# Cross attention computed head by head in 64x64 blocks, and the normalisations moved from VectorE to ScalarE, in a one-core decoder kernel

## What is computed

```python
# self attention, 16 heads of 8 channels, polynomial instead of softmax
att = einsum('bhid,bhjd->bhij', q, k) / sqrt(8); att = where(causal, att, -inf)
att = polymax(att)
x = layernorm(x + (att @ v) @ W_proj)
# cross attention to a context, 16 heads of 64 channels
q = (x @ WQ); k = (ctx @ WK); v = (ctx @ WV)          # 128 -> 1024 each
weights = softmax(einsum('nqhk,nlhk->nhql', q, k) / sqrt(64))
x = layernorm(x + einsum('nhqk,nkhv->nqhv', weights, v).reshape(n, 64, 1024) @ WO + bO)
# 16 experts, the best 6 of them weighted by a router
x = layernorm(x + sum_e gate[:, e] * (x @ expert_w[e]))
```

## Time and profile before

| | |
|---|---|
| median of 3 runs | 1194.37 us (1193.98 to 1194.49) |
| the profiled execution, whole | 1193.11 us |
| its span, first to last instruction | 1191.2 us |
| TensorE busy | 1122.3 us (94%) |
| VectorE busy | 1036.7 us (87%) |
| ScalarE busy | 706.8 us (59%) |
| GpSimd busy | 364.3 us (31%) |
| mean granted TensorE clock | 0.984 of full speed |

### The profile page before, as it was taken

How to read it: one execution, slowest core, us unless ns; L and a number is a source line. 1 busy time by engine, 2 the same in 40 slices (tenths; PEclk the granted TensorE clock), 3 DMA queues, 4 the chain that set the end, 5 groups by cost and what they waited for, 6 DMA issues and landing times.

```text
span 1191.2 us, 31777 instructions
## 1 busy us (share of the span) xinstructions
PE 1122.3 (94%) x9856; PEld 851.6 (71%) x9856; DVE 1036.7 (87%) x3341; ACT 706.8 (59%) x1418; POOL 364.3 (31%) x489
## 2 busy tenths in 40 slices
PE   3989999999999999999999999999999999999964
PEld 3767777777777777777777777777777777777643
DVE  4669998989899988989998898999898999889667
ACT  3766665566675555676555566655666665556420
POOL 3232233232323233232323323332323232332221
PEclk9999999999999999999999999999999999999978
DMA  4232333332233332233333223333322333321230
GB/s 147 59 79 55 94 94 80 92 79 52 67 92 92 79 92 66 52 80 92 92 79 92 56 52 90 92 83 89 83 52 63 92 92 79 92 72 44 63 76 9
DMA packets 49998, 92.09 MB, mean 77 GB/s; under 512 B 6576, under 2 KB 28592, under 8 KB 49968
## 3 DMA queue, kind: packets, MB, share of 16 engines
q1 hardware_dynamic: 49968, 91.70, 31.6%
HBM read 20.37 MB, written 4.19 MB: 21 GB/s over the span
## 4 chain that ended last, share of the span: by engine, by line
PE 56%; DVE 25%; issue 11%; POOL 3%; ACT 2%; DMA 1%; SPq 1%; DVEq 1%; POOLq 0%; ACTq 0%
PE ps_B L370 45%; DVE sums L776 13%; PE ps_S L370 5%; PE ps_B L487 5%; DVE p L723 3%; DVE x L707 3%; POOL rstd L910 2%; DVE ps_B L776 2%; DVE stats L688 1%; DMA vb<-vb_raw 1%; PE ps_B L457 1%; DVE rowmax L719 1%; SPq L354 1%; DVE mv L694 1%; POOL rstd L908 1%
## 5 line engine op out<-in xcount | busy, mean ns | idle before, releaser
L555 ACT ACTIVATE z<-ps_B 128x512 f32<-128x512 f32 x256 | 149.9, 601 | 212.2 <-PE ps_B L370 208.4
L776 DVE SCALAR_TENSOR_TENSOR sums<-ps_B,gate,sums 128x128 f32<-128x128 f32 x896 | 239.5, 341 | 1.4 <-PE ps_B L370 1.4
L915 POOL TENSOR_TENSOR p<-p,rowinv 128x1024 f32<-128x1024 f32 x64 | 122.0, 1906 | 308.6 <-DVE rowinv L732 308.6
L555 ACT ACTIVATE vb_raw<-ps_B 128x512 f32<-128x512 f32 x256 | 155.4, 607 | 88.6 <-PE ps_B L370 69.3
L370 PE MATMUL ps_B<-cT_hi,a_hi 128*128 128x256 f32 x512 | 157.0, 307 | 0.0
L370 PE MATMUL ps_B<-cT_lo,a_hi 128*128 128x256 f32 x512 | 144.2, 282 | 0.0
L370 PE MATMUL ps_B<-cT_hi,a_lo 128*128 128x256 f32 x512 | 144.1, 281 | 0.0
L370 PE MATMUL ps_S<-z,x1T 128*64 128x512 f32 x512 | 126.3, 614 | 10.1 <-DVE p L723 9.5
L370 PE MATMUL ps_B<-ex_hi,x2T_hi 128*128 128x512 f32 x256 | 114.6, 448 | 18.2 <-DVE sums L776 15.4
L370 PEld LDWEIGHTS ps_B<-cT_hi,a_hi 128*128 128x128 f32 x512 | 96.8, 189 | 44.9 <-issue 25.3
L908 POOL TENSOR_TENSOR rstd<-mv,ln_eps_tile 128x2 f32<-128x2 f32 x96 | 18.9, 197 | 337.2 <-DVE mv L694 336.8
(11 more groups left out here) (106 smaller groups left out, 2466.3 us busy)
## 6 DMA issues: line engine op xcount, KB each, us to landing
vb<-vb_raw SPq DMA_DIRECT2D x256, 256.0 KB, 4.3
xT<-in_x_t SPq DMA_DIRECT2D x32, 256.0 KB, 2.6
cT<-in_ctx_t SPq DMA_DIRECT2D x32, 128.0 KB, 2.3
x_sb<-in_x SPq DMA_DIRECT2D x32, 128.0 KB, 3.5
out<-x SPq DMA_DIRECT2D x32, 128.0 KB, 4.1
staging<-in_wq_t SPq DMA_DIRECT2D x1, 512.0 KB, 4.7
staging<-in_wk_t SPq DMA_DIRECT2D x1, 512.0 KB, 5.8
staging<-in_wv_t SPq DMA_DIRECT2D x1, 512.0 KB, 6.7
```

Source lines behind the costliest of these rows:

```text
L555: return nc.scalar.activation(dst, src, ACT.Copy, scale=scale)
L776: done = V.scalar_tensor_tensor(after, ps[BANK[f"FF{4 * r + q}"]][:, C * e:C * e + C], gate[:, r, 4 * q + e:4 * q + e + 1], before, ALU.mu ...
L915: G.tensor_tensor(weights, weights, rowinv[:, r].unsqueeze(2).broadcast_to([P, H, T]), ALU.mult).then_inc(p2_ready, 1)
```

## The change

Nothing is folded any more. Six jobs `heads` transpose WQ, WK and WV once and split them (`heads_hi`, `heads_lo`). For a tile, four jobs `Q2_` form the queries of all heads from `x1T_hi`, `x1T_lo` (stage `l1`), four jobs `K2_` the keys from the context (`l1`), and four jobs `V2_` the values (now in `l2`). The scores are one product for each head and sequence, with 64 channels, 64 queries and 64 keys; the probability product is one for each head and sequence too, and the two sequences' results go to two banks (`AC0a` and `AC0b`). ScalarE moves those four banks to `oT`, and `WO0`, `WO1` multiply by WO. The copies by DMA (`place`) are gone.

ScalarE now does the three `norm` steps as scale and bias; GpSimd's `root` gets two more small instructions for the bias. `x1T` is split by ScalarE (`x1_hi`) and VectorE (`x1_lo`). The value product of self attention writes only the halves that are used. All five orders are new. The diff, cut to its core:

```diff
 ACT_ORDER = """
-    K queries_hi VB6 Y exp0 VB1 Z7 Z2 relu0 relu1 square0 VB3 exp1 VB2 Z5 VB7 PT0a V PT0b square1 Z1 Z0 relu2 Z6
-    relu3 X1T square2 PT1a PT1b square3 VB5 base3 Z4 VB4 X2T Z3 VB0 logit_exp product_hi0 ...
+    Y K queries_hi V2_2 V exp0 V2_3 norm1 V2_0 V2_1 x1_hi exp1 relu0 relu1 K2_0 square0 Q2_0 K2_3 K2_2 PT0a square1
+    relu2 PT0b Q2_2 square2 PT1a PT1b relu3 Q2_1 AC0b square3 AC0a base3 AC1a AC1b norm2 K2_1 X2T Q2_3 logit_exp
+    norm3 heads_hi0 ...
...
 def v():
     for b in range(NB):
-        last = mm(ps[BANK["V"]][:, C * b:C * b + C], xT[:, b].rearrange("p a t -> p (a t)"), w_attn_sb[:, 2 * C:3 * C])
+        for par in range(2):
+            last = mm(ps[BANK["V"]][64 * par:64 * par + 64, T * b:T * b + T], xT[:, b, 0], w_v[:, par])
...
-def vb_part(n):
-    r, par, q = n // 4, n // 2 % 2, n % 2
-    return mm3(ps[BANK[f"VB{n}"]][:], cT_hi[:, rows], cT_lo[:, rows], vo_hi[:, par, cols], vo_lo[:, par, cols])
+def heads_of(what, n, hi, lo):
+    for k in range(2):
+        cols = slice(P * (2 * n + k), P * (2 * n + k) + P)
+        last = mm3(ps[BANK["QKV"[what] + f"2_{n}"]][:, TOK * k:TOK * k + TOK], heads_hi[:, what, cols], heads_lo[:, what, cols], hi[:], lo[:])
+def v2_part(n):
+    rows, cols = slice(P * (n // 2), P * (n // 2) + P), slice(512 * (n % 2), 512 * (n % 2) + 512)
+    return mm3(ps[BANK[f"V2_{n}"]][:], cT_hi[:, rows], cT_lo[:, rows], heads_hi[:, 2, cols], heads_lo[:, 2, cols])
 def s2(r):
-    for q in range(2):
-        for h in range(2):
-            b = 2 * r + h
-            last = mm(ps["S"][64 * h:64 * h + 64, 512 * q:512 * q + 512], x1T[:, T * b:T * b + T],
-                      z[:, b, 8 * q:8 * q + 8].rearrange("p h t -> p (h t)"))
+    pe.sem_inc(heads_begun, 1)
+    for c in range(4):
+        for bpar in range(2):
+            seq = slice(T * (2 * r + bpar), T * (2 * r + bpar) + T)
+            for z in range(2):
+                for e in range(2):
+                    j, cols = 2 * c + z, 512 * e + P * c + T * bpar
+                    last = mm(ps["S"][64 * z:64 * z + 64, cols:cols + T], q2T[64 * e:64 * e + 64, j, seq], k2T[64 * e:64 * e + 64, j, seq])
 def ac(r):
+    pe.sem_inc(heads_begun, 1)
+    for c in range(J):
+        for z in range(2):
+            for bpar in range(2):
+                h = 4 * (c % 4) + 2 * z + c // 4
+                done = mm(ps[own[bpar]][64 * z:64 * z + 64, T * c:T * c + T], v2[64 * bpar:64 * bpar + 64, r, DK * h:DK * h + DK],
+                          p2T[64 * bpar:64 * bpar + 64, r, c, T * z:T * z + T])
+def wo_turn(r):
+    for c in range(J):
+        last = mm(ps[BANK["WO1"]][:, C * r:C * r + C], oT[:, r, c], wo_sb[:, c], c == 0, c == J - 1)
...
+def norm(n):                                  # on ScalarE
+    act.wait_ge(ln_shift[n - 1], tile + 1)
+    for r in range(NR):
+        last = nc.scalar.activation(dst[:, r], rows_of(n, r), ACT.Identity, bias=shift[:, n - 1, r:r + 1], scale=rstd[:, n - 1, r:r + 1])
...
-def norm(n):                                  # on VectorE
-    dve.wait_ge(ln_rstd[n - 1], tile + 1)
-    for r in range(NR):
-        last = V.tensor_scalar(dst[:, r], rows_of(n, r), mv[:, n - 1, r, 0:1], rstd[:, n - 1, r:r + 1], ALU.subtract, ALU.mult)
+def x1T_low():
+    V.scalar_tensor_tensor(x1T_lo[:], ps[BANK["X1T"]][:, 0:TOK], 1.0, x1T_hi[:].bitcast(F32), ALU.mult, ALU.subtract)
...
 def root(n):
     G.tensor_tensor(rstd[:, n - 1], mv[:, n - 1, :, 1], ln_eps_tile[:], ALU.add).then_inc(ln_eps[n - 1], 1)
+    G.tensor_tensor(minus_mean[:, n - 1], mv[:, n - 1, :, 0], minus[:], ALU.mult).then_inc(ln_eps[n - 1], 1)
     G.tensor_tensor(rstd[:, n - 1], rstd[:, n - 1], power[:], ALU.pow).then_inc(ln_rstd[n - 1], 1)
+    G.tensor_tensor(shift[:, n - 1], minus_mean[:, n - 1], rstd[:, n - 1], ALU.mult).then_inc(ln_shift[n - 1], 1)
```

More of the change, by code:

```diff
@@ L81 @@
 SP_ORDER = """
-    x_columns context place1 place0 store x_rows
+    x_columns x_rows store context
 """.split()
 ACT_ORDER = """
-    K queries_hi VB6 Y exp0 VB1 Z7 Z2 relu0 relu1 square0 VB3 exp1 VB2 Z5 VB7 PT0a V PT0b square1 Z1 Z0 relu2 Z6
-    relu3 X1T square2 PT1a PT1b square3 VB5 base3 Z4 VB4 X2T Z3 VB0 logit_exp product_hi0 product_hi1 product_hi2
-    product_hi3 product_hi4 product_hi5 product_hi6 product_hi7
+    Y K queries_hi V2_2 V exp0 V2_3 norm1 V2_0 V2_1 x1_hi exp1 relu0 relu1 K2_0 square0 Q2_0 K2_3 K2_2 PT0a square1
+    relu2 PT0b Q2_2 square2 PT1a PT1b relu3 Q2_1 AC0b square3 AC0a base3 AC1a AC1b norm2 K2_1 X2T Q2_3 logit_exp
+    norm3 heads_hi0 heads_hi1 heads_hi2 heads_hi3 heads_hi4 heads_hi5
 """.split()
 DVE_ORDER = """
[L90 to L94, removed]
+    row_max0 gate2 less_max0 gate3 gate4 projected keys_lo0 gate5 stats1 keys_lo1 var1 queries_lo row_max1 less_max1
+    row_sum0 x1_lo row_inv0 row_sum1 gate6 allow0 row_inv1 pieces0 p1_0 gate7 allow1 gate8 pieces1 allow2 p1_1
+    pieces2 gate9 p1_2 gate10 gate11 gate12 allow3 gate13 pieces3 gate14 p1_3 gate15 weigh0 weigh1 attended stats2
+    var2 weigh2 weigh3 logits stats3 gate0 var3 gate1 heads_lo0 heads_lo1 heads_lo2 heads_lo3 heads_lo4 heads_lo5
 """.split()
 POOL_ORDER = """
-    context_hi context_lo shares0 shares1 root1 root2 next_x_hi bias_x1 next_x_lo x2_hi x2_lo root3 experts_hi
+    root1 next_x_hi context_hi context_lo shares0 shares1 root2 bias_x1 next_x_lo x2_hi root3 x2_lo experts_hi
     experts_lo
@@ L240, in decoder @@
         base3_ready, out_done = sem("base3_ready"), sem("out_done")
-        ln_stats, ln_var, ln_eps, ln_rstd = ([sem(f"ln{n}_{what}") for n in (1, 2, 3)] for what in ("stats", "var", "eps", "rstd"))
-        N_WEIGHTS = 16 * 8
+        ln_stats, ln_var, ln_eps, ln_rstd, ln_shift = ([sem(f"ln{n}_{what}") for n in (1, 2, 3)] for what in ("stats", "var", "eps", "rstd", "shift"))
+        N_WEIGHTS = 16 * (7 + 4)
         def wait(eng, s, n):
@@ L341, in x_columns @@
                         load(xT, x_t, xT_in, u + 1)
[L343 to L354, removed]
                 def store():
@@ L387, in body, with heads, heads_split @@
                 u, t, f = i + 2, i + 1, i - 1
-                def product(n):
+                def heads(n):
                     pe.wait_ge(w_in, N_WEIGHTS)
-                    what, par, q = n // 4, n % 2, n // 2 % 2
-                    rows = slice(64 * par, 64 * par + 64)
-                    left_w, right_w = ((wk_ld, wq_ld), (wv_ld, wo_ld))[what]
                     for k in range(4):
-                        cols = slice(C * (4 * q + k), C * (4 * q + k) + C)
-                        last = mm(ps[BANK[f"product{n}"]][:, C * k:C * k + C], left_w[rows, cols], right_w[rows, cols])
-                    return last
[L401 to L405, removed]
+                        j = 4 * (n % 2) + k
+                        last = pe.transpose(ps[BANK[f"heads{n}"]][:, P * k:P * k + P], heads_ld[n // 2][:, P * j:P * j + P], ident)
+                    return last
+                def heads_split(what):
+                    if isinstance(i, int) and i <= 0:
+                        for n in (2 * what, 2 * what + 1):
+                            wait_emptied(pe, -2, f"heads{n}")
                 def q():
@@ new lines, in s2 @@
+                def s2(r):
+                    wait_moved(f"S2_{r}", i - 1, last_of(ACT_ORDER, [f"Q2_{n}" for n in range(4)]), last_of(ACT_ORDER, [f"K2_{n}" for n in range(4)]))
+                    pe.sem_inc(heads_begun, 1)
[6 more added lines that the diff above has]
+                                    last = mm(ps["S"][64 * z:64 * z + 64, cols:cols + T], q2T[64 * e:64 * e + 64, j, seq], k2T[64 * e:64 * e + 64, j, seq])
@@ L526, in body @@
                         continue
[L528 to L530 removed]
+                    if job == "WO0":
+                        wait(pe, emptied[BANK["WO1"]], earlier(i, "WO1"))
+                    elif job != "WO1":
                         wait(pe, emptied[bank], earlier(i, job))
[L532 to L540 removed]
+                    if job[:2] == "AC":
+                        if job[3] == "b":
+                            ac(int(job[2]))
+                        continue
+                    if job[:2] == "S1":
                         if int(job[3:]) % PARTS == PARTS - 1:
@@ L543, in body @@
                         continue
+                    if job in work:
+                        last = work[job]()
+                    elif job[:2] == "PT":
+                        last = p2_turn(int(job[2]), "ab".index(job[3]))
                     else:
-                        last = ff(int(job[2:]))
+                        last = numbered[job.rstrip("01234567")](int(job[-1]))
                     if bank:
@@ L603, in move_p2T @@
                     move(job, p2T[:, r, 4 * q:4 * q + 4].rearrange("p j n -> p (j n)"), ps[BANK[job]][:])
-                def move_vb(n):
-                    r, par, q = n // 4, n // 2 % 2, n % 2
-                    if f"VB{n}" == first_of(ACT_ORDER, [f"VB{k}" for k in range(4 * r, 4 * r + 4)]):
-                        if not (isinstance(i, int) and t == 0):
```

(4 more changed lines are left out.)

187 lines of the change are left out of this document (85 added, 102 removed), and 23 rows, old and new, of the table JOBS.

## The result

The changed kernel takes 1145.6 us in the median of four runs, against 1194.2 for the kernel before: a ratio of 0.960, with a 95% interval of 0.958 to 0.962. The forecast was 1120 us. So the sign and the range (1080 to 1205) held, and the gain was 49 us where 74 were expected; the likeliest case's own range, 1085 to 1145 us, was just missed. One of the twelve runs of experiment e1, at 1207.7 us, was in a slower state and is left out of its median.

A forecast was written before the change was run, and what follows sets the result against it. TensorE was taken to bound the 35.0 us turn, VectorE close behind; TensorE's terms gave 31.95, plus 0.4 wait and 0.4 by choice, 32.75. Times 32 that is minus 72, setup minus 2: 1120 us, range 1080 to 1205.

The forecast's parts named there:

- the likeliest case: Whole kernel: the forecast itself, 1120 us, with 1085 to 1145 us as its own range; chance 0.62.
- The distance of the 64x64 rows: TensorE's score and probability products: 16.1 ns a row taken, saving 1.68 and 1.59 us a turn.
- two quadrants: Rival on TensorE: only two quadrants overlap, 28.5 ns a small row, 35.5 us a turn, about 1210 us; chance 0.10.
- a floor: Rival on TensorE: small rows have a floor above `Y`'s, 22.3 ns midway, 1160 to 1180 us; chance 0.08.
- no overlap: Rival on TensorE: small rows take 55 ns each, 42.3 us a turn, 1428 us; chance 0.04.
- WO and the values: TensorE, per turn: new WO products plus 3.52 us; four value jobs for eight context jobs minus 2.77.
- the loop: Third `var`, `root`, `norm3`, ScalarE to `square3`, VectorE's `pieces3` and `weigh`, next third `var`: 31.9 us if ScalarE never waits.
- The sum: Per turn: TensorE 31.95 + 0.4, VectorE 32.2, loop 31.9; with 0.4 added, 32.75 us, 2.25 less.
- a new wait: TensorE before `X1T`, for `norm1` on ScalarE behind `Y`, keys and queries: at least 0.2 us, taken as 0.4.
- 0.4 added by choice: Allowance of 0.4 us a turn, because three bounds so near each other will not all be met.
- the rival in which ScalarE's loop binds: Two microseconds of gaps in ScalarE's loop give 34.0 us a turn, about 1160 us; chance 0.12, and 0.04 beyond 1197.
- the two signs of being wrong: TensorE waiting for ScalarE's moves over 2 us a turn, or VectorE idle before `pieces` for a square.

The follow-up runs named there:

- e1: The changed kernel with the third normalisation one turn later in ScalarE's order, behind the next turn's queries; 1194.9 us, ratio 1.002 to the kernel before.
- e8: The changed kernel with two more small GpSimd operations in the third normalisation's `root`, the value unchanged; 1162.4 us, ratio 0.975 to the kernel before.
- e5: The changed kernel with only two of the eight terms of each WO product; 1119.0 us, ratio 0.938 to the kernel before.
- e1b: The changed kernel with the third normalisation behind the next turn's queries and the output store one turn later too; 1139.0 us, ratio 0.956.
- e4: The changed kernel with score and probability products ordered quadrant by quadrant instead of changing quadrant each time; 1403.9 us, ratio 1.177 to the kernel before.

## Why the prediction was right in direction, and where its size was off

*The distance of the 64x64 rows: right.* 16.1 ns was taken, with 14 and 55 as ends; measured up to the next job it is 17. Both jobs of scores and both of probabilities take 1.09 to 1.19 us, 4.46 a turn for 7.39: minus 2.93 where minus 3.27 was expected. A job takes 0.06 us more than `Y`'s 1.03, measured the same way, and the one ahead of `Y`, whose blocks have another size, 0.16 more. The rivals with two quadrants, with a floor and with no overlap did not happen. The Trainium skill's floor (TensorE: Matmul & The Clock Gate, Wait — 56ns, not 53.3ns?) of about 25 ns does not agree with this trace: 17 ns.

*WO and the values: right.* 3.49 us (509.01 to 512.50) for 3.52, and a pass of the value jobs takes 0.24 (523.66 to 523.90). `V` came to 0.62 us (522.71 to 523.33) where 0.46 was expected. Together that makes 2.58 us a turn, not 3.05: mis-sized by 0.47. TensorE's busy time fell by 2.38, from 34.44 to 32.06; the other 0.2 lie between jobs. Behind a job on small blocks the next pass takes 0.33 us (506.81 to 507.14), otherwise 0.23, and a turn has one more stretch of such jobs than before.

*VectorE: nearly right.* Busy 30.9 a turn for 30.3, and it no longer waits for `rstd`.

*The waits and the loop: mis-sized too.* The sum put 0.4 us for a new wait, before `X1T`. That wait is there, and it is 0.40; but `PR` waits 0.64 us for `Y`'s move behind `norm3`, and `X2T` 0.29 for `norm2`, 1.33 together. The text had named the place, `norm3` ahead of `Y`, and gave "more where `norm3` delayed `Y`" no number of its own. It did draw the loop, at 31.9 us, but followed ScalarE all the way down to `square3`. The traced loop leaves ScalarE after `V2_0` and goes through TensorE for 19.3 us, with WO and the probability product in it, which by this reading is why TensorE's rows count there and those beside it, the scores and most of the values among them, do not while this loop is the longest. Its first piece, from the third `var` to `norm3`, was worked out as 1.6 us and is 1.58 (519.36 to 520.94). In the terms of the sum, TensorE's time without work was to be 1.35 us a turn (0.55 as before, 0.4 for the wait, 0.4 added by choice) and is 1.63, and its busy time 31.39 and is 32.06. So of the 0.94 us a turn that the forecast missed, 0.67 are work and 0.28 waits.

*What counted.* Rivals were weighed one against another as if one engine's sum had to win. The outcome, 33.69 us, is nearest to the rival in which ScalarE's loop binds (34.0 us, 1160 us), three quarters of the way to it from the forecast's 32.75, though by another path than the rival had. e8 shows the loop directly, e5 that of 2.7 us fewer TensorE rows only 0.85 count before the next bound, and e1b that a wait of 0.64 us was worth 0.26 for the same reason. That the forecast came as near as it did is in part luck: the 0.4 us added by choice stands for the loop that it had not followed.

*ScalarE and the copies.* Moving the DMA copies away cost nothing, and of the loads only GpSimd's split waits, 3.6 us in total from 300 to 900: right. By the Trainium skill (TensorEngine Tiling (Array Packing), PSUM Bottleneck) the copies out of PSUM may become the bottleneck once the array is tiled. The trace agrees in part: ScalarE is busy 66%, so it is its place in the loop and not its sum that limits.

*The signs.* WO (1.75 us for 16 rows), the rows at 17 ns, VectorE's missing wait for `rstd` and the wait before `X1T` came as named. The turn, 33.69, lies above the 32.3 to 33.3 named. Of the two signs of being wrong, TensorE's waits for ScalarE stay below 2 us (1.33), but VectorE does stand before `pieces` for a square, twice a turn, which it did not before:

```profile
DVE ps_B L748 <- ACT relu L579: 10.1, 36, 0.3
```

*Setup and the ends.* 5.7 us for an expected 2; not taken apart further.

## What to carry to other kernels

Where two or three engines are each busy about 90% of a repeating turn, work out the closed loop (the last step of a turn to the same step one turn later, across all engines) before adding sums for each engine. A delay on a nearly idle engine inside it counts in full (0.53 us for 0.55 here), and a cut on the busiest engine counts only down to the next loop (0.85 us for 2.7 here). So look for the second loop too: here it lay 0.26 us below the first. Moving a step to a less busy engine moves everything queued behind it there, and behind whoever waits for it: in e1 a store held up two loads. Order small products so that neighbours lie in different blocks of the array.

## What the runs showed of the hardware

Float32 products of 64x64 show two rows each. The rows follow each other at 17 ns when each product goes to another quadrant than the one before, and at 52 ns when 16 rows in succession go to the same one (e4): 3.1-fold. With two column halves and 64 columns moving (`V`, 16 rows in 0.62 us) it is 39 ns up to the next job, and 57 ns with 128 moving, where the full array takes 110: 1.9-fold. So the overlap by rows and by columns of the array together gives more than columns alone, and in e4 TensorE did not find it in an order that lacks it.
